# Projection stage: all weight subtractions on VectorE, v's weights loaded one stage earlier, v's copies one tile later on ScalarE

## The chip, the cores and the metric

One core of a Trainium2 chip runs the whole program. The metric is the device time of one launch in microseconds (us). The names of the engines in the profile: PE is TensorE (PEld its weight loads), DVE is VectorE, ACT is ScalarE, POOL is GpSimd, SP is SyncE, which here only issues DMAs.

## The reference, cut to what matters

The program is a two-layer network over x of shape (4, 512, 512): a state-space scan, a mixture of experts, an attention and a quantised MLP, each followed by a residual add and a layer norm. The stage that changes lies between the second and the third part:

```python
x = _layernorm(x + _L0_ffn_ref(x, ...), axis=-1)      # mixture of 16 experts, top 2
# inside _L1_attn_ref:
def proj(w):
    y = jnp.einsum('bsd,ed->bse', x, w)
    return y.reshape(B, S, HEADS, D_K).transpose(0, 2, 1, 3)
q, k, v = (proj(w_q), proj(w_k), proj(w_v))
```

For each of 2048 tokens, the outputs of its two chosen experts are gathered, weighted and added, the sum is normalised, and the result is multiplied by three 512 x 512 matrices. All is float32 to the caller. A float32 product is made of float32r parts (a reduced form that TensorE reads faster): every operand is split into a high part (a rounding copy) and a low part (the operand minus its high part), and three matmuls are added: high x high, high x low, low x high.

## The kernel before, in words

The stages run one after another, each in a block with a barrier at its end: the scan, the first layer norm, routing and the shared experts, the sorted experts (`sorted_experts`), then `normalise_and_project`, and the attention (`attend`). Each engine has an order of its own, written out in the code, and engines meet only through semaphores: an instruction at which an engine waits holds up all that stands behind it on that engine.

**Layout.** The 2048 tokens are 16 tiles (`TILES`) of 128, in four blocks (b) of four tiles. `g.X` and `g.Y` hold the tiles side by side, 16 x 512 floats in a partition. `g.XH` and `g.XL` hold the high and low part of the normalised x, transposed.

**The expert stage** works off 47 sorted tiles (`SORTED`). SyncE loads x tiles and expert weights and stores each tile's result y (`store_y`, L1264) in `sorted_y`; the stores come eight steps behind the loads. The weights land in a ring of seven buffers. Five of them lie inside `g.X`, 1538 floats each, so that ring buffers 5 and 6 lie in the last four tiles of `g.X`. Tile 40 is the last that uses buffer 5, tile 41 the last that uses buffer 6. The y buffers are a ring of four: ScalarE's copy of tile j (`y_copy`, L1372) waits for the store of tile j - 4.

**The projection stage** (L1409) does these steps for each token tile t:

- GpSimd gathers the two expert rows of each token with two indirect DMAs (`gather`, L1508), into a ring of four (`GRING`); the gather of tile t waits until tile t - 4 is added.
- VectorE adds the rows, makes statistics, the inverse root and the centred tile in `g.X` (`add_row`, `stats_of`, `variance`, `inverse_std`, `centre`), and the low part of the transposed tile two tiles later (`low_part`, L1676). ScalarE makes the root (`root`) and the high part (`x_hi`, L1598). TensorE transposes the tile between (L1546).
- TensorE computes *units*. A unit of v is one token tile times v's weights; a unit of q or k is one block of 512 tokens times 128 output columns. Each has 12 matmuls of 512 columns. There are 48: v of block 0 (units 0 to 3), q and k of block 0 (units 4 to 7 and 8 to 11), then q, k and v of each further block. Their results leave through four PSUM banks. ScalarE copies v's product into a padded buffer (`unit`, L1603); of q and k it makes the high part and VectorE the low part, and SyncE stores them, from rings of two buffers.

**The weights.** V, Q, K are numbers 0, 1, 2. The raw weights land in `g.X`: v's where tiles 4 to 7 come later, q's in 8 to 11, k's in 12 to 15. SyncE loads v first, q when tile 0 is added and k when tile 1 is added (L1486). ScalarE makes the high parts, four copies for each (`weights_hi`, L1588): v's first of all, q's after its work on tile 1, k's after its work on tile 3. The low parts of v are made by VectorE ahead of tile 0 (L1643), those of q and k by GpSimd between its gathers (L1517). `centre` of a tile waits until the low parts of the weights that lie in its place are made, and a unit waits for the low parts of its own weights (L1563).

**The padding.** v's buffers lie in `g.Y`, over tiles 0 to 3. GpSimd clears them (`pad`, L1523) when two (four) tiles are centred, and ScalarE's copy of a v product waits for that.

**The orders.** One list, `order` (L1450), places tiles and units: tiles 0, 1, 2, then unit 0, tile 3, unit 1, tile 4, unit 2, tile 5, unit 3, tile 6; from there two units, then one tile. VectorE and ScalarE follow it; on VectorE a unit of v is nothing. TensorE follows it with its transposes of tiles 7 and on placed two units later (`later`, L1462); at entry "tile t" it transposes tile t - 1. On ScalarE the entry "tile t" is the high part of tile t - 2 and the root of tile t.

Of the kernel before, what the change touches and what calls it, by code (L numbers as in the profile page):

```python
# [1197 lines left out]
def sorted_experts(nc, a, g):  # L1198
# [4 lines left out]
    with ExitStack() as ctx:  # L1203
# [42 lines left out]
        @block.sync  # L1246
        def _(sp):
            def load_w(j):
                if j >= RAWS:

                    sp.wait_ge(up_lo, j - RAWS + 1)
                    sp.wait_ge(down_lo, j - RAWS + 1)
                    sp.wait_ge(h_ready, j - RAWS + 1)
                e = nc.values_load(g.owner[0:1, j:j + 1], engines=(mybir.EngineType.SP,), min_val=0, max_val=EXPERTS - 1)
                sp.dma_start(raw[j % RAWS].unsqueeze(1), a["w123"][bass.ds(e, 1)].rearrange("e p w -> p e w")
                             ).then_inc(w_in[j % RAWS], 16)

            def load_x(j):
                if j >= XS:

                    sp.wait_ge(x_turned, j - XS + 1)
                sp.dma_start(x[j % XS][:], g.sorted_x.rearrange("(t p) d -> p t d", p=P)[:, j, :]).then_inc(x_in[j % XS], 16)

            def store_y(j):  # L1264
                sp.wait_ge(y_copied, j + 1)
                sp.dma_start(g.sorted_y.rearrange("(t p) d -> p t d", p=P)[:, j, :], y[j % YS][:]
                             ).then_inc(y_stored[j % YS], 16)

            steps([(0, load_x), (0, load_w), (RAWS + 1, store_y)])
            for k in range(YS):  # L1270
                sp.wait_ge(y_stored[k], 16 * len(range(k, SORTED, YS)))
# [137 lines left out]
def normalise_and_project(nc, a, g):  # L1409

    with ExitStack() as ctx:
# [11 lines left out]
        raw = [g.X[:, KC * (k + 1):KC * (k + 2), :] for k in range(3)]  # L1423
# [7 lines left out]
        w_in = [sem(f"w_in{k}") for k in range(3)]  # L1431
# [43 lines left out]

        def qk_before(u):
# [8 lines left out]
        def _(sp):  # L1485
            for k in (V, Q, K):  # L1486
                if k != V:

                    sp.wait_ge(added, TOP * k)
# [17 lines left out]
        def _(pool):  # L1507
# [9 lines left out]
            def weights_lo(n, c):  # L1517
                k = (Q, K)[n]
                pool.wait_ge(w_hi, KC * k + c + 1)
                nc.gpsimd.tensor_tensor(wl[k][:, c, :], raw[k][:, c, :], wh[k][:, c, :].bitcast(F32),  # L1520
                                        ALU.subtract).then_inc(w_lo, 1)

# [7 lines left out]
            for t in range(GRING):  # L1530
                gather(t)
            pad(0)
            for t in range(GRING, TILES):
                gather(t)
                if t == GRING:
                    pad(1)
                if t < GRING + 4:
                    for c in range(2 * (t % 2), 2 * (t % 2) + 2):
                        weights_lo((t - GRING) // 2, c)
# [47 lines left out]
        def _(act):  # L1587
            def weights_hi(k):  # L1588
                act.wait_ge(w_in[k], 16)
                for c in range(KC):  # L1590
# [31 lines left out]
            weights_hi(V)  # L1622
            due = None
            for kind, k in order:
# [11 lines left out]
                if k in (1, 3):  # L1636
                    weights_hi((Q, K)[k // 2])

        @block.vector
        def _(dve):  # L1640
            nc.vector.memset(eps[:], EPS).then_inc(eps_ready, 1)

            def v_weights_lo(c):  # L1643
                dve.wait_ge(w_hi, c + 1)
                nc.vector.tensor_tensor(wl[V][:, c, :], raw[V][:, c, :], wh[V][:, c, :].bitcast(F32),
                                        ALU.subtract).then_inc(v_lo, 1)

# [14 lines left out]
            def centre(m):  # L1662
                dve.wait_ge(rstd_ready, m + 1)
                if KC <= m < 2 * KC:

                    dve.wait_ge(v_lo, KC)
                elif m >= 2 * KC:
                    dve.wait_ge(w_lo, KC * (m // KC - 1))
# [39 lines left out]
            for c in range(KC):  # L1708
                v_weights_lo(c)
            for kind, k in order:  # L1710
                (tile if kind == "tile" else unit)(k)

# [762 lines left out]
def program(nc, a, out):  # L2475
# [7 lines left out]
    with ExitStack() as ctx:  # L2483
        sb, _, sem = scoped(nc, ctx, "all")
        g.scattered, g.gathered = sem("scattered"), [sem(f"gathered{k}") for k in range(4)]
        g.ident = sb("ident", [P, P])
# [107 lines left out]
```

## Time and profile before

| | us |
|---|---|
| median of 3 timed runs | 2047.34 |
| lowest and highest | 2046.64, 2048.67 |
| the profiled execution, its own time | 2044.7 |
| its span, first to last instruction | 2042.8 |
| TensorE busy (share of the span) | 1730.1 (85%) |
| VectorE busy | 1560.9 (76%) |
| ScalarE busy | 832.8 (41%) |
| GpSimd busy | 771.0 (38%) |

Times in the rows are microseconds from the start of the span. The expert stage ends, and the projection stage starts, between 823 and 826.5; the attention begins at 1004.9. A timeline row has the start, the duration, the engine, the line, the operation, the tile written and the tiles read, the shape, and the number of instructions that were merged. In square brackets stands the engine's idle time before it and who ended it. TensorE's matmuls overlap, so the start of the next one tells its pace better than its duration. PEclk is the granted clock as a share of 2.4 GHz: 1.00 is 2.4 GHz and 0.50 is 1.2 GHz.

### The profile page before, as it was taken

The numbers are of one execution on the slowest core, as the hardware profiler recorded it, in microseconds if no ns is written. First come the engines' busy times: TensorE is split into PE (matmuls) and PEld (weight loads), VectorE is DVE, ScalarE is ACT, GpSimd is POOL, SyncE is SP. The second block draws the span as 40 slices with busy tenths as digits, with TensorE's granted clock in tenths as the row PEclk, the third lists the DMA queues.
The fourth block names the chain that finished last, engine by engine and source line by source line (L and its number), as shares of the span: only waits on it lengthen the run. The fifth ranks groups of instructions, "written<-read, shape, count | busy, mean of one in ns | idle before, by whom it ended". The sixth has DMA issues, their size and how long they took to land. (4 is left out here: it accounts for less than half of the span.)

```text
span 2042.8 us, 24785 instructions
## 1 busy us (share of the span) xinstructions
PE 1730.1 (85%) x7795; PEld 1048.7 (51%) x7795; DVE 1560.9 (76%) x2835; ACT 832.8 (41%) x1400; POOL 771.0 (38%) x471
## 2 busy tenths in 40 slices
PE   5888879776668899399678888889879999999997
PEld 1232323223346787288523333333557787778786
DVE  6999999999624999463278888886786667766678
ACT  4646464443111677332146777777211111111112
POOL 4897989894060999440113000000004213321200
PEclk7999989999779999799879999999999999999999
DMA  4334242321040998574543333331001000000002
GB/s 134 99 108 127 85 135 82 103 83 37 8 165 26 405 411 350 182 251 186 174 122 104 89 94 93 94 94 27 1 7 56 32 1 32 31 5 28 1 1 83
DMA packets 110651, 211.58 MB, mean 104 GB/s; under 512 B 18889, under 2 KB 35657, under 8 KB 109627
## 3 DMA queue, kind: packets, MB, share of 16 engines
q1 hardware_dynamic: 105403, 193.23, 28.9%
q0 software_dynamic: 5120, 16.78, 2.4%
q8 instruction: 64, 1.05, 0.2%
q14 instruction: 64, 0.52, 0.1%
HBM read 144.87 MB, written 62.65 MB: 102 GB/s over the span
## 5 line engine op out<-in xcount | busy, mean ns | idle before, releaser
L1992 DVE TENSOR_REDUCE att_top<-att_first 128x1 f32<-128x512 f32 x512 | 332.3, 686 | 69.4 <-PE att_first L1872 62.0
L551 DVE TENSOR_TENSOR_SCAN ssm_h<-ssm_da,ssm_dbx 128x512 f32<-128x512 f32 x256 | 305.3, 1210 | 6.3 <-ACT ssm_da L421 6.1
L291 POOL TENSOR_TENSOR ssm_dbx<-ssm_u,ssm_bbc 128x2048 f32<-128x2048 f32 x63 | 285.3, 4529 | 47.6 <-DVE ssm_h L551 47.2
L634 PE MATMUL ssm_y<-ssm_hc,all_ident 128*128 128x512 f32 x396 | 226.3, 659 | 76.0 <-DVE ssm_hc L502 70.4
L1954 ACT ACTIVATE att_prob<-att_second 128x1024 f32<-128x1024 f32 x256 | 248.1, 1022 | 86.3 <-PE att_second L1892 81.0
L421 ACT ACTIVATE ssm_da<-ssm_dt,ssm_minus_a 128x512 f32<-128x512 f32 x256 | 176.7, 690 | 200.4 <-DVE ssm_h L551 200.2
L2246 POOL TENSOR_TENSOR pairs_raw<-pairs_raw,pairs_scales 128x512 f32<-128x512 f32 x42 | 42.3, 1042 | 503.2 <-DMA pairs_raw<-in_w 503.2
L2376 ACT ACTIVATE ffn_silu<-ffn_pg 128x256 f32<-128x256 f32 x112 | 43.1, 385 | 408.4 <-PE ffn_pg L129 408.4
L1872 PE MATMUL att_first<-att_ks,att_qs 48*128 48x512 f32 x512 | 133.3, 510 | 65.5 <-DVE att_top L1992 50.6
L127 PE MATMUL ffn_pg<-pairs_wh,last_XH 128*128 128x512 f32 x448 | 177.6, 396 | 1.7 <-PEq L2050 1.7
L128 PE MATMUL ffn_pg<-pairs_wl,last_XH 128*128 128x512 f32 x448 | 177.6, 396 | 0.0
L129 PE MATMUL ffn_pg<-pairs_wh,last_XL 128*128 128x512 f32 x448 | 176.0, 393 | 0.0
L634 PEld LDWEIGHTS ssm_y<-ssm_hc,all_ident 128*128 128x128 f32 x396 | 64.5, 198 | 188.1 <-DVE ssm_hc L502 133.8
L1872 PEld LDWEIGHTS att_first<-att_ks,att_qs 48*128 48x128 f32 x512 | 53.5, 190 | 194.6 <-DVE att_top L1992 133.5
L2400 DVE TENSOR_TENSOR ffn_h<-ffn_pg,ffn_silu 128x256 f32<-128x256 f32 x112 | 47.4, 423 | 131.0 <-ACT ffn_silu L2376 130.9
L502 DVE TENSOR_TENSOR ssm_hc<-ssm_cbc,ssm_h 128x512 f32<-128x512 f32 x198 | 132.2, 668 | 14.4 <-issue 7.1
L1907 PE MATMUL att_out<-att_prob,att_v 128*32 128x512 f32 x1024 | 137.1, 608 | 0.1
L2253 POOL TENSOR_SCALAR pairs_wh<-pairs_raw 128x512 fp32r<-128x512 f32 x42 | 24.9, 623 | 235.2 <-PE ffn_py L129 235.2
L127 PE MATMUL ffn_py<-pairs_wh,ffn_hh 128*128 128x512 f32 x224 | 97.9, 437 | 0.2 <-DVE ffn_hl L2418 0.2
L127 PEld LDWEIGHTS ffn_pg<-pairs_wh,last_XH 128*128 128x128 f32 x448 | 85.0, 190 | 22.3 <-issue 2.0
L1892 PE MATMUL att_second<-att_qs,att_ks 56*128 56x512 f32 x512 | 92.2, 415 | 3.7 <-DMA att_qs<-att_rows 1.9
L129 PEld LDWEIGHTS ffn_pg<-pairs_wh,last_XL 128*128 128x128 f32 x448 | 85.1, 190 | 19.3
(311 smaller groups left out, 3780.5 us busy)
## 6 DMA issues: line engine op xcount, KB each, us to landing
all_X<-in_w SPq DMA_DIRECT2D x33, 769.0 KB, 9.1
ssm_bbc<-brow_dram SPq DMA_DIRECT2D x64, 256.0 KB, 4.2
ssm_cbs<-crow_dram SPq DMA_DIRECT2D x58, 256.0 KB, 3.4
mlps_raw<-in_w SPq DMA_DIRECT2D x16, 769.0 KB, 8.6
att_qs<-qk_dram SPq DMA_DIRECT2D x192, 64.0 KB, 2.2
att_ks<-qk_dram SPq DMA_DIRECT2D x192, 64.0 KB, 2.2
sorted_x<-ssm_zero SPq DMA_DIRECT2D x47, 256.0 KB, 3.6
exp_x<-sorted_x SPq DMA_DIRECT2D x47, 256.0 KB, 9.5
```

Of the source, the lines that this page charges most:

```text
L127: pe.matmul(out, lh, rh, start=first, stop=False)
L128: pe.matmul(out, lh, rl, start=False, stop=False)
L129: return pe.matmul(out, ll, rh, start=False, stop=last)
L291: nc.gpsimd.tensor_tensor(dbx[:, n % 2], u[:, n // STATE % 2], bbc[:, n % RING, :].unsqueeze(1).to_broadcast([P, KC, NB]), ALU.mult).then_ ...
L421: nc.scalar.activation(da[:, i % 2, :], dt[:, b % 2, c, :], ACT.Exp, scale=minus_a[:, c, n % STATE:n % STATE + 1]).then_inc(da_ready, 1)
L502: nc.vector.tensor_tensor(hc[:, k % 2, :], cbc[:], h[:, n % 2, c, :], ALU.mult).then_inc(hc_ready, 1)
L551: nc.vector.tensor_tensor_scan(h[:, n % 2, c, :], da[:, i % 2, :], dbx[:, n % 2, c, :], 0.0, ALU.mult, ALU.add).then_inc(h_ready, 1)
L634: pe.matmul(y[:, c, :], g.ident[:], hc[:, k % 2, :], start=(m == 0), stop=(m == STATE - 1)).then_inc(y_own, 1)
L1872: pe.matmul(p_first[first_place(m) % FIRSTS][:], qs[w % RING][at, pair, qt * P:(qt + 1) * P], ks[w % RING][at, pair, :], start=True, stop= ...
L1907: mm = pe.matmul(p_out[VPAD * j:VPAD * (j + 1), :], v[s % RING][:, kt, VPAD * j:VPAD * (j + 1)], prob[step % 2][:, j, :], start=(kt == 0), ...
L1954: nc.scalar.activation(prob[step % 2][:, js, :], p_second[second_place(step, pair) % 2][:], ACT.Exp, scale=DK ** -0.5).then_inc(exp_done, 1)
L1992: nc.vector.tensor_reduce(top[w % 2][:, qt, item:item + 1], p_first[first_place(m) % FIRSTS][:], AX.X, ALU.max).then_inc(max_done, 1)
```

## The change

GpSimd loses its subtractions and only gathers and pads. Its order becomes: all gathers in turn, with the two pads behind gathers 4 and 5. VectorE makes the low parts of all three weights: v's and q's ahead of tile 0, k's in pairs after tiles 6 and 7. v's weights now lie in tiles 12 to 15 of `g.X` and are loaded in the expert stage, ahead of the store of tile 41; a semaphore that lives through all stages tells that they have landed. q's lie in tiles 4 to 7 and are loaded first in the projection stage, k's in 8 to 11 and when tile 0 is added. ScalarE makes v's and q's high parts ahead of everything, and k's one chunk at a time after tiles 3 to 6. On ScalarE alone, each of the first four units trades places with the tile behind it in the order.

```diff
--- before.py
+++ after.py
@@ -1261,7 +1261,16 @@
                     sp.wait_ge(x_turned, j - XS + 1)
                 sp.dma_start(x[j % XS][:], g.sorted_x.rearrange("(t p) d -> p t d", p=P)[:, j, :]).then_inc(x_in[j % XS], 16)
 
+            def load_next(last):
+                sp.wait_ge(up_lo, last + 1)
+                sp.wait_ge(down_lo, last + 1)
+                sp.wait_ge(h_ready, last + 1)
+                sp.dma_start(g.X[:, 3 * KC:4 * KC, :], a["wqkvT"][2].rearrange("(c p) e -> p c e", p=P)
+                             ).then_inc(g.v_landed, 16)
+
             def store_y(j):
+                if j == SORTED - 6:
+                    load_next(j)
                 sp.wait_ge(y_copied, j + 1)
                 sp.dma_start(g.sorted_y.rearrange("(t p) d -> p t d", p=P)[:, j, :], y[j % YS][:]
                              ).then_inc(y_stored[j % YS], 16)
@@ -1420,7 +1429,7 @@
         eps = sb("eps", [P, 1])
         rows = sb("rows", [P, GRING, TOP, DIM])
 
-        raw = [g.X[:, KC * (k + 1):KC * (k + 2), :] for k in range(3)]
+        raw = [g.X[:, KC * k:KC * (k + 1), :] for k in (3, 1, 2)]
         wh, wl = ([sb(f"{n}{k}", [P, KC, DIM], F32R) for k in range(3)] for n in ("wh", "wl"))
         hi = sb("hi", [P, 2, NB], F32R)
         lo = sb("lo", [P, 2, NB], F32R)
@@ -1428,7 +1437,7 @@
         v = [g.Y[:, 2 * k:2 * k + 2, :].rearrange("p t (h d) -> p (t h) d", d=VPAD) for k in range(2)]
         pt = [ps(f"pt{k}", [P, KC, P]) for k in range(2)]
         po = [ps(f"po{k}", [P, NB]) for k in range(4)]
-        w_in = [sem(f"w_in{k}") for k in range(3)]
+        w_in = [g.v_landed] + [sem(f"w_in{k}") for k in (Q, K)]
         w_hi, v_lo, w_lo, pads, product = sem("w_hi"), sem("v_lo"), sem("w_lo"), sem("pads"), sem("product")
         added, stats_ready, var_ready, std_ready = sem("added"), sem("stats_ready"), sem("var_ready"), sem("std_ready")
         eps_ready, rstd_ready, x_ready, x_turned = sem("eps_ready"), sem("rstd_ready"), sem("x_ready"), sem("x_turned")
@@ -1473,6 +1482,14 @@
                     out.append(("tile", held.pop(0)[1]))
             return out + [("tile", k) for _, k in held]
 
+        def after_tile(entries):
+
+            out = list(entries)
+            for u in range(PER_BLOCK):
+                i = out.index(("unit", u))
+                out[i], out[i + 1] = out[i + 1], out[i]
+            return out
+
         def qk_before(u):
             return sum(kind != V for kind, _, _ in units[:u])
 
@@ -1483,10 +1500,10 @@
 
         @block.sync
         def _(sp):
-            for k in (V, Q, K):
-                if k != V:
-
-                    sp.wait_ge(added, TOP * k)
+            for k in (Q, K):
+                if k == K:
+
+                    sp.wait_ge(added, TOP)
                 sp.dma_start(raw[k], a["wqkvT"][SOURCE[k]].rearrange("(c p) e -> p c e", p=P)).then_inc(w_in[k], 16)
             for u, (kind, b, c) in enumerate(units):
                 if kind == V:
@@ -1514,12 +1531,6 @@
                                                  bass.IndirectOffsetOnAxis(g.at[:, k, t:t + 1], 0)
                                                  ).then_inc(g.gathered[t % GRING], 16)
 
-            def weights_lo(n, c):
-                k = (Q, K)[n]
-                pool.wait_ge(w_hi, KC * k + c + 1)
-                nc.gpsimd.tensor_tensor(wl[k][:, c, :], raw[k][:, c, :], wh[k][:, c, :].bitcast(F32),
-                                        ALU.subtract).then_inc(w_lo, 1)
-
             def pad(k):
 
                 pool.wait_ge(x_ready, 2 * k + 2)
@@ -1527,16 +1538,10 @@
                 pool.wait_ge(pads, 2 * k + 1)
                 nc.gpsimd.memset(v[k][:, :, DK:DK + 1], 1.0).then_inc(pads, 1)
 
-            for t in range(GRING):
+            for t in range(TILES):
                 gather(t)
-            pad(0)
-            for t in range(GRING, TILES):
-                gather(t)
-                if t == GRING:
-                    pad(1)
-                if t < GRING + 4:
-                    for c in range(2 * (t % 2), 2 * (t % 2) + 2):
-                        weights_lo((t - GRING) // 2, c)
+                if t in (GRING, GRING + 1):
+                    pad(t - GRING)
 
         @block.tensor
         def _(pe):
@@ -1585,9 +1590,9 @@
 
         @block.scalar
         def _(act):
-            def weights_hi(k):
+            def weights_hi(k, chunks=range(KC)):
                 act.wait_ge(w_in[k], 16)
-                for c in range(KC):
+                for c in chunks:
                     nc.scalar.activation(wh[k][:, c, :], raw[k][:, c, :], ACT.Copy).then_inc(w_hi, 1)
 
             def root(t):
@@ -1620,8 +1625,9 @@
 
             act.wait_ge(eps_ready, 1)
             weights_hi(V)
+            weights_hi(Q)
             due = None
-            for kind, k in order:
+            for kind, k in after_tile(order):
                 if kind == "unit":
                     unit(k)
                     if due is not None:
@@ -1633,8 +1639,8 @@
                     due = k
                 else:
                     root(k)
-                if k in (1, 3):
-                    weights_hi((Q, K)[k // 2])
+                if 3 <= k < 3 + KC:
+                    weights_hi(K, [k - 3])
 
         @block.vector
         def _(dve):
@@ -1644,6 +1650,11 @@
                 dve.wait_ge(w_hi, c + 1)
                 nc.vector.tensor_tensor(wl[V][:, c, :], raw[V][:, c, :], wh[V][:, c, :].bitcast(F32),
                                         ALU.subtract).then_inc(v_lo, 1)
+
+            def weights_lo(k, c):
+                dve.wait_ge(w_hi, KC * k + c + 1)
+                nc.vector.tensor_tensor(wl[k][:, c, :], raw[k][:, c, :], wh[k][:, c, :].bitcast(F32),
+                                        ALU.subtract).then_inc(w_lo, 1)
 
             def add_row(t, k):
                 if k == 0:
@@ -1661,11 +1672,11 @@
 
             def centre(m):
                 dve.wait_ge(rstd_ready, m + 1)
-                if KC <= m < 2 * KC:
-
+                if KC <= m < 3 * KC:
+
+                    dve.wait_ge(w_lo, KC * (m // KC))
+                elif m >= 3 * KC:
                     dve.wait_ge(v_lo, KC)
-                elif m >= 2 * KC:
-                    dve.wait_ge(w_lo, KC * (m // KC - 1))
                 nc.vector.tensor_scalar(g.X[:, m, :], g.Y[:, m, :], mv[:, m, 0:1], rstd[:, m:m + 1], ALU.subtract,
                                         ALU.mult).then_inc(x_ready, 1)
 
@@ -1707,8 +1718,13 @@
 
             for c in range(KC):
                 v_weights_lo(c)
+            for c in range(KC):
+                weights_lo(Q, c)
             for kind, k in order:
                 (tile if kind == "tile" else unit)(k)
+                if kind == "tile" and k in (6, 7):
+                    for c in range(2 * (k - 6), 2 * (k - 6) + 2):
+                        weights_lo(K, c)
 
 
 def attend(nc, a, g):
@@ -2483,6 +2499,7 @@
     with ExitStack() as ctx:
         sb, _, sem = scoped(nc, ctx, "all")
         g.scattered, g.gathered = sem("scattered"), [sem(f"gathered{k}") for k in range(4)]
+        g.v_landed = sem("v_landed")
         g.ident = sb("ident", [P, P])
         g.gate = sb("gate", [P, MLPS, TILES])
```

## Rows read from the trace of the kernel before

**Rows 1.** Busy time by stage: length, engines' busy us (count), clock, DMA share, GB/s.
```profile
848.20:872.80 24.60, 17.11 (x60) 12.97 (x61) 12.89 (x26) 6.52 (x14) 15.27 (x15) 0.79 0.35 118
872.80:1001.20 128.40, 128.32 (x573) 103.38 (x571) 53.89 (x101) 35.10 (x67) 17.52 (x18) 1.00 0.59 216
```

**Rows 2.** Timeline, from the first weights to the start of unit 0.
```profile
833.21 2.19 ACT L1591 ACTIVATE proj_wh<-all_X 128x512 fp32r<-128x512 f32 x4 [10.26 <-DMA all_X<-in_wqkvT]
...
833.87 2.50 DVE L1645 TENSOR_TENSOR proj_wl<-all_X,proj_wh 128x512 fp32r<-128x512 f32 x4 [6.90 <-ACT proj_wh L1591]
834.75 1.24 POOL L1513 DMA_INDIRECT proj_rows<-sorted_y,all_at  x1 [0.31 <-issue]
...
836.29 1.53 DVE L1654 SCALAR_TENSOR_TENSOR all_sums<-proj_rows,all_weight,all_sums 128x512 f32<-128x512 f32 x2
...
843.64 0.69 DVE L1674 BATCH_NORM_STATS2 proj_stats<-all_sums 128x6 f32<-128x512 f32 x1
...
844.70 2.19 ACT L1591 ACTIVATE proj_wh<-all_X 128x512 fp32r<-128x512 f32 x4 [2.71 <-DMA all_X<-in_wqkvT]
...
846.79 0.57 ACT L1601 ACTIVATE later_XH<-proj_pt 128x512 fp32r<-128x512 f32 x1
847.40 0.69 DVE L1679 TENSOR_TENSOR later_XL<-proj_pt,later_XH 128x512 fp32r<-128x512 f32 x1 [3.06 <-ACT later_XH L1601]
...
848.24 0.76 PE L127 MATMUL proj_po<-proj_wh,later_XH 128*128 128x512 f32 x1 [4.12 <-DVE later_XL L1679]
```

**Rows 3.** Timeline, from unit 0 to unit 3.
```profile
851.36 0.46 PE L128 MATMUL proj_po<-proj_wl,later_XH 128*128 128x512 f32 x1
...
852.59 0.60 PE L1552 MATMUL proj_pt<-all_ident,all_X 128*128 128x128 f32 x4
...
853.28 0.59 ACT L1601 ACTIVATE later_XH<-proj_pt 128x512 fp32r<-128x512 f32 x1
...
854.74 0.47 PE L127 MATMUL proj_po<-proj_wh,later_XH 128*128 128x512 f32 x1 [1.55 <-DVE later_XL L1679]
...
856.04 0.96 POOL L1526 MEMSET all_sums<- 128x1024 f32 x1 [9.54 <-DVE all_X L1669]
...
864.75 0.75 DVE L1654 SCALAR_TENSOR_TENSOR all_sums<-proj_rows,all_weight,all_sums 128x512 f32<-128x512 f32 x1 [5.03 <-DMA proj_rows<-sorted_y,all_at]
...
868.28 0.77 PE L127 MATMUL proj_po<-proj_wh,later_XH 128*128 128x512 f32 x1 [0.95 <-DVE later_XL L1679]
```

**Rows 4.** Timeline, from the first q unit to the first k unit.
```profile
873.20 0.48 PE L127 MATMUL proj_po<-later_XH,proj_wh 128*128 128x512 f32 x1
...
880.31 0.74 DVE L1654 SCALAR_TENSOR_TENSOR all_sums<-proj_rows,all_weight,all_sums 128x512 f32<-128x512 f32 x1
...
883.70 0.66 DVE L1705 TENSOR_TENSOR proj_lo<-proj_po,proj_hi 128x512 fp32r<-128x512 f32 x1
...
884.47 0.60 PE L1552 MATMUL proj_pt<-all_ident,all_X 128*128 128x128 f32 x4
884.83 0.48 PE L127 MATMUL proj_po<-later_XH,proj_wh 128*128 128x512 f32 x1
```

**Rows 5.** DMA issues: count, KB each, median us to landing; projection, projection, expert stage.
```profile
all_X<-in_wqkvT SPq DMA_DIRECT2D x3, 1024.0 KB, 6.7
proj_rows<-sorted_y,all_at POOLq DMA_INDIRECT x32, 3.9
...
sorted_y<-exp_y SPq DMA_DIRECT2D x47, 256.0 KB, 9.1
```

**Rows 6.** Timeline, end of the expert stage.
```profile
805.52 0.34 DVE L1393 SCALAR_TENSOR_TENSOR exp_h<-exp_pr,all_X,exp_silu 128x128 f32<-128x128 f32 x1
...
807.07 0.32 SPq L1266 DMA_DIRECT2D sorted_y<-exp_y  x1
...
820.87 0.58 ACT L1377 ACTIVATE exp_y<-exp_py 128x512 f32<-128x512 f32 x1
```

**Rows 7.** VectorE's low part of h in the expert stage: ns min/median/max, first and last start.
```profile
L1403 DVE TENSOR_TENSOR exp_hl<-exp_h,exp_hh x47: 292/1123/1366, 675.0 to 821.0; 128x128 fp32r<-128x128 f32 x47
```

## The prediction

> **What bounds the kernel now.** I read the stage table first. In the projection stage TensorE is without a pause from 872.8 us to the end of the stage: 128.32 busy us of 128.40 at a granted clock of 1.00. In the 24.6 us before that it is busy 17.11 us at a mean clock of 0.79 [rows 1]. So the last 128 us are TensorE's own work, and the only time to be had lies ahead of the first q unit, which starts at 873.20 [rows 4]. The view of waits for this stage then names the engines to follow: ScalarE waits for the weight loads, and GpSimd for VectorE's centred tiles, before it may pad v. The timeline shows what this does to TensorE. Three things hold it up:
>
> (a) Unit 0 (v of token tile 0) starts at 848.24, right behind the low part of tile 0 (VectorE, 847.40), which waits for ScalarE's high part of it (846.79). This one stands behind ScalarE's four copies of q's weights (844.70), which wait for q's load [rows 2]. VectorE was ready for this low part much sooner: its statistics of tile 2, the operation just ahead in its order, start at 843.64.
>
> (b) The high part of tile 1 starts at 853.28. It stands behind the copy of unit 0's product, although its transposes were done at 844.1 in the same timeline; unit 1 starts only at 854.74, 2.15 us after the transposes that follow unit 0 (852.59) [rows 3].
>
> (c) GpSimd's second pad begins at 856.04 after 9.54 us of waiting, and two of its own subtractions follow. The gather of tile 5 comes behind all this, VectorE gets its rows at 864.75 after 5.03 us idle, and unit 3 starts at 868.28, on a TensorE that has idled and begins at the low clock again [rows 3].
>
> **What stays: the start.** Before, v's load is issued first in the stage; after, q's stands in that place. The copies start 833.21 when the first load has landed, the subtractions follow from 833.87, and the first row addition starts at 836.29 [rows 2]. The same three steps now run on q's weights, so tile 0 starts at 836.3 again. v's own copies and subtractions (2.19 us and 2.50 us [rows 2]) run in the empty stretch between the barrier and 833, because v has landed long before. Added to VectorE ahead of tile 0: four subtractions, hidden by q's load in the sense that v's old four stood exactly there. If that cover were gone, it would be 2.5 us. K's load is issued after tile 0 is added, as q's was; it lands at about 844.7, and its first copy is wanted only at 848.8.
>
> **v's load in the expert stage.** It waits for three counts of tile 41; the last, its gated product, starts at 805.52, and SyncE has issued the store of tile 40 at 807.07 [rows 6]. So it issues at 807.4 and adds no wait to SyncE; the store of tile 41 behind it waits anyway for a later copy. The queue then holds 1 MB ahead of the stores of tiles 41 to 46. The first of these to be missed is tile 41's: its buffer is written again by the copy of tile 45, at 820.87 [rows 6]. With loads in flight such a store took 9.1 us median [rows 5]; issued at 810.4 it lands at 819.5. Cost 0; upper bound, if it took 2 us more than that, 0.6 us.
>
> **(a) removed.** ScalarE's copies of q no longer stand between it and tile 0. The transposed tile 0 lies ready from about 841.3 (the timeline has its transposes at 840.11 to 841.22), its high part runs at 842.0 behind the root of tile 1, so VectorE takes the low part directly after its statistics of tile 2, at 843.64 + 0.61 = 844.25. Unit 0 starts 0.84 us after the low part's start, as before (848.24 − 847.40): 845.09, 3.15 us earlier. It takes 4.35 us (848.24 to 852.59), since the clock is low in it until 851.36, its eighth matmul [rows 2, 3].
>
> **(b) and (c) removed.** From here I rolled the stage forward with two periods. VectorE, one tile without a wait: 880.31 to 883.70 = 3.4 us. TensorE, a unit at full clock: (884.83 − 873.20) holds four units and one set of transposes; the transposes take 0.36 of it (884.47 to 884.83), so a unit is 11.27 / 4 = 2.82, and unit plus transposes 3.18 [rows 4]. TensorE: transposes 849.44, unit 1 849.80, unit 2 852.98, unit 3 856.16, transposes 858.98, first q unit 859.34. VectorE: tile 3 at 844.95, tile 4 at 848.35, tile 5 at 851.75. Low parts 1, 2 and 3 are done at 848.3, 851.8 and 855.1, each before its unit. Low part 2 is the tightest: ScalarE takes unit 0's copy at 849.6, tile 2's high part at 850.1 to 850.7, VectorE wants it at 851.05. ScalarE's added work per tile, one K copy of 0.55 (2.19 / 4 [rows 2]), fits in its slack.
>
> GpSimd: gather 4 from 837.9 (no longer behind a pad), first pad 843.0, gather 5 at 844.2, which lands by 849.4 and is wanted at 851.75. The second pad waits for tile 3 to be centred, 849.7, and ends at 850.9; gather 6 is issued till 853.1. Landing took 3.9 us median [rows 5], so from the second issue at 852.2 it is there at 856.1. VectorE wants it at 855.15: a new wait of 0.9 us. Tile 5's transposes need VectorE's centring at 857.5 and stand at 858.98, so it costs TensorE nothing; the cover is 1.5 us.
>
> Shift of the first q unit: 873.20 − 859.34 = 13.9 us.
>
> **K's subtractions on VectorE.** Two after tile 6 (859.4 to 860.7) lie in time it has free. The two after tile 7 are on a path: relative to the first q unit, VectorE leaves tile 7 at 883.70 − 873.20 = 10.5; two subtractions take 1.3 (four took 2.50), and the semaphore 0.15, so K's low parts stand at 11.95. TensorE comes to the first k unit at 884.83 − 873.20 = 11.63 [rows 2, 4]. A new stall of 0.3 us; bounds 0 (VectorE leaves tile 7 sooner) and 1 us. Removing GpSimd's eight subtractions saves only its own time, already counted in (c).
>
> Behind that the order of work is as before and TensorE has no gap, so nothing is given back. Sum: 13.9 − 0.3 = **13.6 us**. Terms in doubt: unit 0 wholly at the low clock (matmuls started every 3.12 / 7 = 0.446 us there, 12 of them 5.35 instead of 4.35) −1.0; a late landing of gather 6 −0.6; the next stages' phase against the clock and the queues ±1.
>
> The profiled execution took 2044.7 us around a span of 2042.8; I expect 2031.1 of its counterpart. It lies 2.6 below the median of the timed runs, 2047.34, and the difference is taken from that: **2033.7 us**.
>
> **A rule on the shared port.** In the expert stage VectorE's 128x128 subtraction took 1123 ns median and 292 at the least [rows 7], the least where GpSimd had finished; so the two engines do hold each other up. The Trainium skill, "SBUF — State Buffer", section "SBUF: two separate sides", says that this port pair is an exclusive lock, and that a VectorE operation holding it keeps GpSimd from writing the descriptors of its transfers. That speaks against moving the subtractions beside the gathers. Here one gather issue beside v's four subtractions took 1.24 us (834.75) [rows 2], against 0.95 of its neighbours there. By the rule each of some 12 issues beside a subtraction would lose up to 0.7 us, by the row 0.3. Only gather 6 has no slack, and no moved subtraction stands beside it.
>
> **Rivals.**
> 1. *Unit 0 is not released by ScalarE.* Everything of (a), 3.15 us, stays; the rest goes. 2047.34 − 10.5 = 2036.9. Against it: the three starts, 846.79, 847.40 and 848.24, follow each other directly [rows 2]. 6%.
> 2. *The clock stays low through units 1 to 3.* TensorE now has idle time between the first transposes and unit 0. Each unit would take 5.35 instead of 2.82: 3 x 2.53, and four sets of transposes 0.4 each more: 9 us lost, 2043. Before, it rose 3.1 us into unit 0 and stayed up over a pause of 1.5 us [rows 2, 3]. 4%.
> 3. *Gathers starve behind VectorE* (the port lock as a mechanism of this kernel): GpSimd's issues grow by 0.7 each, gather 6 comes 1.4 us later and the first k unit waits 1 us. 2047.34 − 12.0 = 2035.3. The 1.24 us issue speaks for a third of this. 6%.
> 4. *Slower: the stores become the bound.* Pulled forward, the q and k stores meet the gathers in a tighter stretch, and with a ring of two buffers ScalarE and then TensorE wait. The engines' queues were busy 0.59 of 128.40 us, 76 us [rows 1]. The same work would have to take more than 128.4 + 13.6 = 142 us of queue before the kernel gets slower, and 146 before it shows: 2052 at that point. Nearly double the transfer time for the same bytes; little speaks for it. 3%.
> 5. *The change doesn't do what it says*: v's load holds the last expert tiles, or tile 0 starts later as q's load lands late, up to all of the gain. 2047. Against it: all three loads landed in 6.6 to 6.8 us, 6.7 median [rows 5]. 3%.
>
> **Chances.** The forecast 78%, with its own range 2032 to 2036. 0.2% is 4 us, about what a measurement of this kernel can tell from no change. Faster by over that: forecast, rivals 1 and 3, most of 2, = 94%; within it 3%; slower 3%. The range is 2031 to 2037.5: below it only phase effects, above it rival 2, 4 and 5.
>
> **What would show it.** The first row addition still at 836.3; ScalarE's high part of tile 0 near 842.0 and unit 0 at 845.1; unit 1 about 849.8; no idle before units 2 and 3; gather 6's rows awaited for about 0.9 us; first q unit at 859.3; a TensorE wait of about 0.3 us on K's subtractions near 871; the stage ended near 987.5. If unit 0 starts at 848, the first step is wrong; if the first addition is later than 836.5, the start is; if the first q unit is early and the span is not, something behind the stage took it back.

## The result, and the profile after

The changed kernel took 2031.99 us (median of 4 runs, 2030.60 to 2034.81) against 2046.99 (4 runs, 2046.03 to 2048.67): ratio 0.9928, 95% interval 0.9915 to 0.9941, that is 15.0 us less, 12 to 17. The forecast was 2033.7, in a range of 2031 to 2037.5. The profiled execution took 2031.32 us around a span of 2029.5; its counterpart before, 2044.7 and 2042.8.

The stage table of the changed kernel, with the columns of [rows 1]. The first row begins inside unit 0. TensorE is busy in all of it, where it had 17.11 of 24.60 us; of the second row it lacks one pause ahead of the first k unit (870.08, below) and the last 2.1 us, which come after the stage's last matmul:

```profile
845.20:860.00 14.80, 14.80 (x72) 12.06 (x71) 12.55 (x26) 6.53 (x14) 9.44 (x11) 0.97 0.72 230
860.00:988.50 128.50, 125.73 (x559) 101.07 (x557) 54.59 (x101) 34.18 (x65) 10.94 (x12) 1.00 0.58 212
```

The timeline of the changed kernel, from the first weights to the first k unit; its lines answer to [rows 2 to 4]:

```profile
826.37 2.19 ACT L1596 ACTIVATE proj_wh<-all_X 128x512 fp32r<-128x512 f32 x4 [3.96 <-DVE proj_eps L1647]
...
831.42 2.19 ACT L1596 ACTIVATE proj_wh<-all_X 128x512 fp32r<-128x512 f32 x4 [2.87 <-DMA all_X<-in_wqkvT]
...
834.50 1.53 DVE L1665 SCALAR_TENSOR_TENSOR all_sums<-proj_rows,all_weight,all_sums 128x512 f32<-128x512 f32 x2
...
840.11 0.58 ACT L1606 ACTIVATE later_XH<-proj_pt 128x512 fp32r<-128x512 f32 x1
...
842.47 0.67 DVE L1690 TENSOR_TENSOR later_XL<-proj_pt,later_XH 128x512 fp32r<-128x512 f32 x1
...
843.29 0.77 PE L127 MATMUL proj_po<-proj_wh,later_XH 128*128 128x512 f32 x1 [0.95 <-DVE later_XL L1690]
...
847.49 0.60 PE L1557 MATMUL proj_pt<-all_ident,all_X 128*128 128x128 f32 x4
847.85 0.48 PE L127 MATMUL proj_po<-proj_wh,later_XH 128*128 128x512 f32 x1
...
854.69 0.75 DVE L1665 SCALAR_TENSOR_TENSOR all_sums<-proj_rows,all_weight,all_sums 128x512 f32<-128x512 f32 x1 [1.37 <-DMA proj_rows<-sorted_y,all_at]
...
857.57 0.48 PE L127 MATMUL proj_po<-later_XH,proj_wh 128*128 128x512 f32 x1
...
861.25 0.60 ACT L1617 ACTIVATE all_sums<-proj_po 128x512 f32<-128x512 f32 x1 [2.24 <-PE proj_po L129]
...
868.72 1.26 DVE L1656 TENSOR_TENSOR proj_wl<-all_X,proj_wh 128x512 fp32r<-128x512 f32 x2
...
868.85 0.60 PE L1557 MATMUL proj_pt<-all_ident,all_X 128*128 128x128 f32 x4
870.08 0.47 PE L127 MATMUL proj_po<-later_XH,proj_wh 128*128 128x512 f32 x1 [0.64 <-issue]
```

The reader sees v's weights copied at 826.37, at once; the low part of tile 0 directly behind VectorE's statistics; no bracket on any TensorE line between 843.29 and 868.85; and one new wait, at 870.08, for which the profile names no releaser (x5 finds it).

Executions start the stage at other times (825.8 here, 826.5 before, near 811 in the later runs), so from here on times count from the stage's first DMA issue. "First gating copy" is ScalarE's first copy of the weights whose subtractions stand last ahead of tile 0 (v's in the kernel before and in x4, q's elsewhere; none where only v's, loaded long before, stand there). A unit's column is the start of its first matmul. The last column is the stage, from its first issue to the attention's first. Each row is one profiled execution.

| kernel (trace) | first gating copy | tile 0 added | unit 0 | unit 1 | unit 2 | unit 3 | first q unit | first k unit | stage |
|---|---|---|---|---|---|---|---|---|---|
| before | 6.74 | 9.82 | 21.77 | 28.27 | 33.31 | 41.81 | 46.73 | 58.36 | 178.39 |
| changed | 5.59 | 8.67 | 17.46 | 22.02 | 25.26 | 28.50 | 31.74 | 44.25 | 164.28 |
| changed, again (x0) | 7.32 | 10.51 | 19.30 | 24.29 | 27.53 | 30.76 | 34.00 | 45.86 | 165.88 |
| changed, third (x9) | 5.70 | 8.77 | 17.56 | 23.04 | 26.28 | 29.51 | 32.74 | 44.61 | 164.63 |
| x1 plain order | 5.61 | 8.68 | 17.48 | 24.93 | 29.97 | 34.99 | 38.23 | 50.10 | 170.13 |
| x2 GpSimd subtracts | - | 6.88 | 15.68 | 20.25 | 24.14 | 34.50 | 39.83 | 51.46 | 171.50 |
| x3 v loaded late | 12.24 | 15.32 | 24.11 | 29.90 | 33.14 | 36.38 | 39.61 | 51.48 | 171.64 |
| x4 before, ScalarE's order | 5.69 | 8.77 | 21.60 | 27.15 | 30.39 | 42.54 | 47.88 | 59.52 | 179.55 |
| x5 k behind tile 6 | 5.72 | 8.80 | 17.59 | 23.17 | 26.41 | 29.64 | 32.87 | 44.51 | 164.55 |
| x6 pad later | 7.42 | 10.53 | 19.32 | 23.96 | 27.21 | 30.44 | 33.67 | 45.54 | 165.56 |
| x7 q later | - | 6.94 | 15.74 | 21.28 | 24.52 | 27.76 | 31.00 | 42.63 | 162.66 |
| x10 q later, again | - | 6.97 | 15.77 | 20.40 | 23.65 | 27.33 | 30.57 | 42.20 | 162.24 |
| x8 extra GpSimd work | 6.90 | 9.97 | 18.76 | 23.65 | 26.88 | 33.37 | 39.33 | 51.27 | 171.31 |

Of the 15.0 us between the first q units (46.73 − 31.74), 14.1 are left at the stage's end.

### The profile page after: what moved, and what is told of

Same layout as the page of the kernel before. It is cut to its first block and busy times, and to the rows that moved or that the text cites. A ratio compares the mean times of both kernels' runs of the same rounds, so it can differ in the third digit from the quotient of the medians.

```text
span 2029.5 us, 24786 instructions
## 1 busy us (share of the span) xinstructions
PE 1731.3 (85%) x7795; PEld 1050.6 (52%) x7795; DVE 1564.8 (77%) x2843; ACT 831.9 (41%) x1400; POOL 759.5 (37%) x463
## 3 DMA queue, kind: packets, MB, share of 16 engines
q8 instruction: 65, 1.06, 0.2%
## 5 line engine op out<-in xcount | busy, mean ns | idle before, releaser
L502 DVE TENSOR_TENSOR ssm_hc<-ssm_cbc,ssm_h 128x512 f32<-128x512 f32 x198 | 131.7, 665 | 14.1 <-issue 7.1
```

What stands on the lines that cost most here:

```text
L502: nc.vector.tensor_tensor(hc[:, k % 2, :], cbc[:], h[:, n % 2, c, :], ALU.mult).then_inc(hc_ready, 1)
```

## The experiments

Timed ratios are against the kernel before on the same chip. Those of x0 and x5 to x10 come from later, faster chip time, in which the kernel before took 2028.7 and 2029.6 us.

**x1: ScalarE in the plain order.**
```diff
-            for kind, k in after_tile(order):
+            for kind, k in order:
```


> The changed kernel, with ScalarE following the plain order again (unit 0's copy ahead of tile 1's high part, and so on). Theory (the order on ScalarE is worth one copy in the loop of each of units 1 to 3): before, a unit started 2.15 us after the transposes ahead of it, now 0.36, so 1.8 us each, 5.4 us at the first q unit (857.57 to about 863.0), and 2037.4 us in all against 2032.0. Rival (VectorE's row period of 3.4 us is the real limit and the copy lies in its shadow): first q unit within 1 us of 857.6, 2032 to 2033.

2039.27 us, ratio 0.9965 (0.9952 to 0.9978). TensorE's lines of this kernel:
```profile
845.38 0.77 PE L127 MATMUL proj_po<-proj_wh,later_XH 128*128 128x512 f32 x1 [0.95 <-DVE later_XL L1690]
...
850.63 0.89 PE L1557 MATMUL proj_pt<-all_ident,all_X 128*128 128x128 f32 x4
852.83 0.47 PE L127 MATMUL proj_po<-proj_wh,later_XH 128*128 128x512 f32 x1 [1.30 <-DVE later_XL L1690]
...
857.87 0.47 PE L127 MATMUL proj_po<-proj_wh,later_XH 128*128 128x512 f32 x1 [1.55 <-DVE later_XL L1690]
```
Unit 0 starts where it did (17.48); units 1 to 3 again stand about 2.2 us behind the transposes ahead of them. The first q unit slipped 6.5 us: 1.8 x 3, and 1.05 because unit 0 took 5.25 us here (845.38 to 850.63) against 4.20. The 1.05 is not the order's: in x9, unedited, unit 0 took 5.13. The rival falls.

**x2: GpSimd subtracts again,** in its old order; v's prefetch and ScalarE's order stay.
```diff
...
-            for c in range(KC):
-                weights_lo(Q, c)
...
+            pad(0)
+            for t in range(GRING, TILES):
+                gather(t)
+                if t == GRING:
+                    pad(1)
+                if t < GRING + 4:
+                    for c in range(2 * (t % 2), 2 * (t % 2) + 2):
+                        weights_lo((t - GRING) // 2, c)
...
```


> The changed kernel, with GpSimd making the low parts of q and k again, between pads and gathers in its order of before; loads and ScalarE as changed. Theory: gather 5 comes behind the second pad and two subtractions (2.5 us), lands near 858 where VectorE wants it at 851, unit 3 starts near 861.3 instead of 854.3, TensorE idles over 5 us and loses clock for another 0.5 to 1.5 us; first q unit near 865, no stall at the first k unit; 2039 us, 7 more. Rival (the pads alone, not the subtractions, held the gathers): 2.5 us or less.

2038.27 us, ratio 0.9954 (0.9937 to 0.9972). Its gather 5 and TensorE behind it:
```profile
857.99 0.75 DVE L1677 SCALAR_TENSOR_TENSOR all_sums<-proj_rows,all_weight,all_sums 128x512 f32<-128x512 f32 x1 [6.88 <-DMA proj_rows<-sorted_y,all_at]
...
859.45 1.11 PE L1569 MATMUL proj_pt<-all_ident,all_X 128*128 128x128 f32 x4 [5.24 <-DVE all_X L1692]
861.52 0.76 PE L127 MATMUL proj_po<-proj_wh,later_XH 128*128 128x512 f32 x1 [0.96 <-DVE later_XL L1702]
```
As expected: VectorE waits 6.88 us, unit 3 starts at 861.5, and it begins at the low clock. The first k unit follows the first q unit at 11.63, without a stall. It showed something else too: with no subtraction of q ahead of it, tile 0 starts at 6.88 instead of 8.67, and what it waits for there is its gather. The four subtractions of q cost 1.8 us where the change put them.

**x3: v's load in the projection stage.**
```diff
-                if j == SORTED - 6:
-                    load_next(j)
...
-            for k in (Q, K):
+            for k in (V, Q, K):
```


> The changed kernel, with v's load issued first in the projection stage instead of in the expert stage, q's right behind it. Theory: two loads of 1 MB share the queues with the gathers, q lands 2.5 to 4 us later than now (831.4), the first row addition moves from 834.5 to 837 to 838.5, and all behind it by as much: 2035 us, 3 more. It also shows the 1.1 us by which q's load landed sooner than v's had. Rival (VectorE would wait for the gathers anyway): under 1 us.

2041.28 us, ratio 0.9963 (0.9949 to 0.9977). Direction right, size wrong: 7.9 us at the first q unit, not 3. Of these, unit 0 starts 6.65 later, and 1.06 is unit 0 itself, which took 5.26 us here against 4.20, as it can in the unedited kernel (x9). ScalarE's copies of v and of q in this kernel:
```profile
832.48 2.19 ACT L1594 ACTIVATE proj_wh<-all_X 128x512 fp32r<-128x512 f32 x4 [9.07 <-DMA all_X<-in_wqkvT]
...
839.06 2.19 ACT L1594 ACTIVATE proj_wh<-all_X 128x512 fp32r<-128x512 f32 x4 [4.39 <-DMA all_X<-in_wqkvT]
```
The two loads, issued back to back, did not share the time here; the second came 6.6 us behind the first. V's load also landed in 5.66 us here though it stood first as before, where it took 6.74: the sooner landing is not the change's.

**x4: the kernel before with ScalarE's order alone.**
```diff
-            for kind, k in order:
+            for kind, k in after_tile(order):
```


> The kernel before, with the one edit of ScalarE's order. Theory: unit 0 stays at 848.2, unit 1 starts 1.8 us sooner; its larger effect is that tile 3 is centred 3 us sooner, so the second pad and gather 5 come 3 us sooner (VectorE gets its rows near 861.7 instead of 864.75), units 3 and on by as much: 2044.0 us, 3 less than before. The parts of the change then don't add up as 5.4 and the rest. Rival (gather 5 sits behind something else): 0 to 1 us less.

2047.38 us, ratio 0.9991 (0.9978 to 1.0004): nothing, where 3 us were expected. The rows of gather 5 did come sooner (36.05 against 38.28), and units 1 and 2 too, but the first q unit came later (47.88 against 46.73). Two lines of VectorE, and GpSimd's beside them:
```profile
862.83 3.51 DVE L1677 TENSOR_SCALAR all_X<-all_sums,proj_mv,proj_rstd 128x512 f32<-128x512 f32 x1
...
868.32 3.19 DVE L1662 SCALAR_TENSOR_TENSOR all_sums<-proj_rows,all_weight,all_sums 128x512 f32<-128x512 f32 x1
```
```profile
862.13 1.40 POOL L1521 DMA_INDIRECT proj_rows<-sorted_y,all_at  x1 [0.30 <-issue]
863.56 2.48 POOL L1528 TENSOR_TENSOR proj_wl<-all_X,proj_wh 128x512 fp32r<-128x512 f32 x2
```
A centring took 3.51 us, six times its 0.55. It began during a gather's issue (862.13 to 863.53) and ended at 866.34, just behind the two subtractions that followed (863.56 to 866.04). This accounts for the missing gain: the rows came 2.23 us sooner, the centring of tile 4 behind the first of them took 2.96 longer, and the transposes ahead of unit 3 wait for it, so unit 3 starts 0.73 later (42.54 against 41.81); from there to the first q unit it takes 0.42 more, as the clock rose later in unit 3. The row addition at 868.32 (0.74 elsewhere) began in the next gather's issue and was held in the same way.

**x8: the same put on purpose.** The changed kernel with four unused subtractions behind gather 6:
```diff
+                if t == GRING + 2:
+                    pool.wait_ge(w_hi, KC)
+                    for c in range(KC):
...
+                        nc.gpsimd.tensor_tensor(extra[:, c % 2, :], wh[V][:, c, :].bitcast(F32), ...,
+                                                ALU.subtract).then_inc(extras, 1)
```


> The changed kernel, with four subtractions that nobody uses added on GpSimd behind gather 6, two SBUF operands of 128x512 each, beside VectorE's tiles 5 and 6. In the trace of the kernel before with ScalarE's order alone changed, one of VectorE's centrings took 3.51 us (0.55 elsewhere) and one row addition 3.19 us (0.74), both beginning just ahead of a pair of GpSimd's subtractions and ending with it. Theory (GpSimd's two-operand operations lock VectorE's SBUF operations out until a row of them ends): at least one centring, row addition or both here takes 1.3 to 5 us, the same operations elsewhere in the stage their usual 0.55 and 0.74, and the first q unit slips by 0 to 4 us. Rival (it was something else, the gathers' descriptors for one): all stay at 0.55 and 0.74 as in the unedited changed kernel. Later gathers come 5 us later, which their lead covers.

One execution: span 2021.6 us, against 2014.5 and 2015.7 of the unedited changed kernel there. The timeline of this kernel, VectorE and GpSimd together:
```profile
838.24 0.95 POOL L1531 DMA_INDIRECT proj_rows<-sorted_y,all_at  x1 [0.30 <-issue]
...
838.44 5.07 DVE L1688 TENSOR_SCALAR all_X<-all_sums,proj_mv,proj_rstd 128x512 f32<-128x512 f32 x1
...
839.20 4.02 POOL L1551 TENSOR_TENSOR proj_extra<-proj_wh 128x512 f32<-128x512 f32 x4
```
The centring again began in a gather's issue and ended (843.51) only behind the fourth subtraction (843.22). Between the gather and the subtractions GpSimd left 0.01 us, and VectorE did not get in between two subtractions either. The first q unit came 5.4 us later, counted from unit 0 (20.57 against 15.18 of x9). The theory holds in kind; both sizes lie above what was expected (5.07 against at most 5, 5.4 against at most 4). It is a matter of phase: x2 has the same eight subtractions as x4, and all its centrings took 0.55.

How many of GpSimd's operations VectorE has to wait out is not settled, for the expert stage of the kernel before shows it held by one alone:
```profile
806.12 2.03 POOL L1280 TENSOR_SCALAR mlps_wh<-all_X 128x1024 fp32r<-128x1024 f32 x1
...
807.16 1.12 DVE L1403 TENSOR_TENSOR exp_hl<-exp_h,exp_hh 128x128 fp32r<-128x128 f32 x1
...
808.11 1.33 POOL L1285 TENSOR_TENSOR later_XL<-mlps_raw,later_XL 128x512 fp32r<-128x512 f32 x1
```
The subtraction (0.29 us where GpSimd is done) ended at 808.28, 0.13 behind the operation in which it began, although GpSimd's next one followed at once. What makes the difference to x4 and x8, where it began in a gather's issue, no run shows.

**x5: k's subtractions behind tile 6.**
```diff
-                if kind == "tile" and k in (6, 7):
-                    for c in range(2 * (k - 6), 2 * (k - 6) + 2):
+                if kind == "tile" and k == 6:
+                    for c in range(KC):
```


> The changed kernel, with all four of k's subtractions behind tile 6 on VectorE, where it idled 4.8 us, instead of two behind tile 6 and two behind tile 7. Theory (the stall of 0.87 us ahead of the first k unit is k's last low part): the stall goes, first k unit 11.6 us behind the first q unit instead of 12.5, 2031.1 us. Rival (ScalarE's late high part of the first q unit holds something else too): the stall stays or turns up at another unit, 2032.

2018.35 us, ratio 0.9945 (0.9931 to 0.9958). From the first q to the first k unit it takes 11.64 us, as before the change (11.63): the stall is gone, so it was k's last low part. The total doesn't show it: it is 3.5 us above x0's, the attention of this trace is 3.3 longer than that of x0 (403.1 against 399.8), and the bounds are wider than the effect. The expected gain in time is not shown.

**x6: the second pad behind gather 6.**
```diff
-                if t in (GRING, GRING + 1):
-                    pad(t - GRING)
+                if t in (GRING, GRING + 2):
+                    pad((t - GRING) // 2)
```


> The changed kernel, with the second pad behind gather 6 instead of ahead of it. Theory: gather 6 comes 2.5 us sooner or more, VectorE's wait of 1.37 us before tile 6 goes, and TensorE's starts stay within 0.2 us: that wait was covered, 2032.0 us. Rival (it costs, through tile 5's transposes or the stores): 0.5 to 1.4 us faster. Also watched: whether ScalarE's pause of 2.2 us before the copy of unit 3 shrinks, as it must if the store of v's tile 1 was held up by the row of gathers behind the second pad.

2018.07 us, ratio 0.9947 (0.9932 to 0.9962). VectorE waits for no gather any more, and TensorE's steps from unit 1 on are the same 3.23 to 3.25: the wait was covered. ScalarE copies unit 3 without a pause:
```profile
845.73 0.60 ACT L1617 ACTIVATE all_sums<-proj_po 128x512 f32<-128x512 f32 x1
848.96 0.60 ACT L1624 ACTIVATE proj_hi<-proj_po 128x512 fp32r<-128x512 f32 x1 [2.64 <-PE proj_po L129]
```
This doesn't come from the pad alone: counted from the first q unit, x5, with the pad where the change has it, makes this copy as soon (0.15 us ahead of it in both), while x0 and x9 make it 0.8 and 1.2 later, of which nothing reached the first k unit, and the first trace 3.8 later. That the gathers held up the store of v's tile 1 in the first trace is argued, not shown.

**x0, x7, x9, x10: the unedited changed kernel (x0, x9), and one that uses what x2, x5 and x6 showed (x7, x10).** The latter has x6's pad too, and each centring of tiles 4 to 7 waits only for the low part that lies in its place.
```diff
...
-            for c in range(KC):
-                weights_lo(Q, c)
...
+                if kind == "tile" and k in (3, 4, 5):
+                    for c in ((0,), (1,), (2, 3))[k - 3]:
+                        weights_lo(Q, c)
+                if kind == "tile" and k == 6:
+                    for c in range(KC):
+                        weights_lo(K, c)
```


> The changed kernel once more, unedited, beside the three below on one chip. If the first load's landing (5.6 us in its trace, 6.7 in the trace of before) and the attention stage's length (402.0 us from its first to its last first product, 399.7 before) vary from execution to execution, both differ here again by a few tenths to 2 us; if they belong to the change, they stay at 5.6 and 402. The first k unit's stall of 0.9 us comes back either way. 2032 us.

> The changed kernel, with q's subtractions no longer ahead of tile 0 but behind tiles 3, 4 (one each) and 5 (two), all of k's behind tile 6, the second pad behind gather 6, and centring of tiles 4 to 7 waiting only for the low part that lies in its place. Theory (q's load and its subtractions set tile 0's start at 8.67 us from the stage's first issue; with only the gathers to wait for it was 6.88): all units 1.8 us sooner, VectorE's slack of 1.1 to 2.5 us behind TensorE just covers the four subtractions, and the stall at the first k unit goes: 2.6 us in all, 2029.4 us. Rival (VectorE becomes the bound of units 2 to 4): units 2, 3 and the first q unit slip back by up to 2.5 us, no gain but the 0.9 us, 2031.

> The changed kernel, unedited, as the measure for the one below on the same chip. The stage's length from its first issue to the attention's: 164.3 and 165.9 us in two traces so far, first load landed in 5.6 and 7.3 us; here one of the two again, ratio 0.993.

> The kernel with q's subtractions behind tiles 3 to 5 and k's behind tile 6 once more, against the changed kernel on the same chip. Theory (its stage is 1.6 to 3.2 us shorter, as in the one trace, 162.7): ratio lower than the changed kernel's by 0.0008 to 0.0016. Rival (the rest of the program takes it back, or the stage varies by as much): no difference, as the medians of 2014.8 and 2014.9 had it; the stage's length in the trace tells the two apart.

The changed kernel: 2014.86 us, ratio 0.9930 (0.9914 to 0.9945), and 2015.73, 0.9932 (0.9914 to 0.9950). The edited one: 2014.80, 0.9932 (0.9918 to 0.9945), and 2017.55, 0.9938 (0.9926 to 0.9950). In the traces the theory holds: tile 0 at 6.9, no stall at the first k unit, a stage of 162.7 and 162.2 us, 1.6 to 3.6 less than the three traces of the changed kernel. In time there is no difference, and the expected 2.6 us isn't there. The attention behind it, from its first to its last first product, took 399.6 to 403.1 us in all traces of these experiments, without regard to the edit (399.8 and 399.6 for the changed kernel, 400.0 and 401.3 for the edited one; 399.7 before and 402.0 in the first trace after), which is as large as the gain. Whether it takes the gain back or merely hides it is open. So no version is shown to beat the changed kernel.

## Why the prediction was right

**The start (predicted: the same).** Right as a mechanism: q's weights took v's place and tile 0 started 3.1 us behind their first copy, as before (9.82 − 6.74 = 3.08; 8.67 − 5.59 = 3.08). The size of the landing was taken from one execution. It was 6.74 there, and 5.59, 7.32 and 5.70 in three traces of the changed kernel, 5.69 in x4 with the loads of before. This is worth 1.15 of the 15.0 us in the traces and is no part of the change. It also hid a choice: q's subtractions need not stand there (x2).

**(a), 3.15 us.** From tile 0's addition to unit 0: 11.95 before, 8.79 after, 3.16 less. Shown by the ScalarE line at 840.11, and the same 8.79 in x0 and x9; no run puts q's copies back to where they stood, so the step is read from traces and not taken back alone. Rival 1 fell.

**(b) and (c).** From unit 0 to the first q unit: 24.96 before, 14.28 after, 10.68 less, to 0.03 us the forecast's (859.34 − 845.09 = 14.25). So close a hit is luck: unit 0 took 4.20 us and not 4.35, each step of transposes and unit 3.24 and not 3.18, and in x0 and x9 the same stretch took 14.70 and 15.18. What differs there is unit 0, by when the clock rises in it: here after the sixth matmul, one sooner than before, in x0 after the eighth, in x9 only at its last (4.63 and 5.13 us). The prediction had this as a term in doubt, 1.0 us. From unit 1 on the clock stayed up: rival 2 fell in every trace of the changed kernel. The edits are not a sum of parts: taken back singly, ScalarE's order cost 6.5 us at the first q unit, GpSimd's subtractions 8.1 and v's load 7.9, together 22.5 for a change of 15. Set against x9, whose unit 0 has the slower clock as theirs in x1 and x3, it is 5.5, 7.1 and 6.9, together 19.5 for 14.0; added singly, ScalarE's order gave nothing.

**v's load in the expert stage, cost 0.** It was issued at 807.03, and the stage behind it began 825.83, no later than before. Its price was seen from the wrong side: I did not price what it saved, since q took its place; x3 says 6.6 us of load and 7.9 in all, 1.06 of it the clock in unit 0.

**Gather 6, a covered wait of 0.9 us.** It was 1.37, 1.02 and 1.41, and covered (x6).

**K's subtractions, a stall of 0.3 us.** 12.51 − 11.63 = 0.88 in the first trace, 0.23 and 0.24 in the two others, 0 in x5. As the usual size the term was right; the first trace has 0.65 more, and there ScalarE stood idle for 2.24 us ahead of unit 3's copy (861.25) and VectorE's tile 7 came 0.64 later than in x0 and x9, counted from the first q unit. The DMA view of the changed kernel between 859 and 862 (packets, MB, share of the 16 engines' time) has them with the gathers (q0) and hardly with the stores (q1):
```profile
q0 software_dynamic: 310, 1.04, 90.3%
q1 hardware_dynamic: 33, 0.09, 7.5%
```

**Rival 3, the port.** The moved subtractions slowed no gather enough to matter: issues took 0.94 to 1.31 us, 1.28 beside k's second pair. But the lock was weighed in one direction only, VectorE against GpSimd's issues. The larger price lay in the other, VectorE's operations behind GpSimd's (x4, x8), and the change removes its cause. The Trainium skill, "SBUF — State Buffer", section "SBUF: two separate sides", has whichever operation starts first hold the pair for its whole instruction and the other block fully; of VectorE's it names those in a two-port mode, which also starve the descriptors, and those with two SBUF inputs. The moved subtractions are of the second kind, so the 0.7 us an issue that the prediction worked out by the rule is more than the page states. The expert stage's row at 807.16 agrees with the page, held for one operation; x4 and x8 go beyond it, with 3.51 and 5.07 us behind two and four subtractions in a row. The trace of before had no such centring (545 to 549 ns), so none of the 15 us is due to it.

**Rival 4, the stores.** The queues were busy 0.58 of the long stretch, 0.59 before, and TensorE had no pause but the one at 870.08.

Two errors in part cancelled in the stage: 1.15 us more at the start, 0.6 more of stall, 14.1 where 13.6 were forecast. The profiled executions differ by 13.4 us: the stage ended 14.75 sooner in the span, the attention took 2.3 longer and the rest 0.9 less. The medians differ by 15.0 us here and by 13.9 and 13.8 in the repetitions x0 and x9, so the forecast's 13.6 stands better than the first pair alone would say. Of the kernel before there is one trace only, so how much of its start and its clock is chance isn't known.

## What to carry to other kernels

Roll each engine's own order forward with its period, and ask for each copy or subtraction not only what it costs but what stands behind it in that order: 0.6 us of copying set 1.8 us a unit, and two subtractions held a gather by 2.5. Trying one part of such a change alone can mislead: ScalarE's order alone won 2.2 us at gather 5 and lost them to a centring that GpSimd held. Take GpSimd's two-operand SBUF work away from a VectorE that is near the critical path, even where the trace at hand shows no harm: the price comes by phase, and in x4 and x8 it was two and four of its operations in a row. Repeat the trace before explaining a difference of 1 us: a load's landing and the clock in unit 0 each moved by that much in the same kernel.

## What the runs showed of the hardware

- A VectorE centring of 0.55 us took 3.51 and 5.07 us when it began inside a gather's issue that GpSimd followed at once with two and four subtractions (x4, x8), and a row addition of 0.74 took 3.19 (x4). In the expert stage a subtraction of 0.29 took 1.12, held by one GpSimd operation and not by the next.
- The stage's first load of 1 MB landed, by the copy that waits for it, after 5.6 to 7.4 us in thirteen traces: 5.6 to 5.7 in nine and 6.7 to 7.4 in four, both among the three traces of the changed kernel. In the one trace with a second load right behind it, that came 6.6 us after the first (x3).
- Unit 0, twelve matmuls that begin at the low clock (granted 0.50 of 2.4 GHz), took 4.20 to 5.26 us, by when the clock rose in it; unit 1 behind it, at 1.00, took 2.89 (847.85 to 850.74).
